# A two-layer graph network on 128 graphs: the last B round of each quad on ScalarE and GpSimd

## What is computed

```python
def L0(x, adj, W1, b1, W2, b2):
    mask = (adj > 0.0)
    W1a, W1b = W1[:F], W1[F:]
    diff = x[:, :, None, :] - x[:, None, :, :]
    h = relu((x @ W1a)[:, :, None, :] + diff @ W1b + b1)     # 192 wide
    hm = einsum('bjkh,bjk->bjh', h, mask)
    return hm @ W2 + mask.sum(-1)[..., None] * b2
def L1(h, A, ...):
    m = relu(relu(h @ W1 + b1) @ W2 + b2)
    msg = relu(einsum('bij,bjh->bih', A, m))
    r, z = sigmoid(i_r + h_r), sigmoid(i_z + h_z)            # of msg @ W_ih, h @ W_hh
    return (1 - z) * tanh(i_n + r * h_n) + z * h
x = layernorm(x + L0(x, adj, ...))
x = layernorm(x + L1(x, adj, ...))
```

## Time and profile before

| | us |
|---|---|
| median of 3 runs | 966.77 (965.92 to 966.85) |
| the profiled execution | 966.09 |
| its span, first to last instruction | 964.4 |
| TensorE busy | 852.2 (88%) |
| VectorE busy | 870.5 (90%) |
| ScalarE busy | 568.0 (59%) |
| GpSimd busy | 314.7 (33%) |
| mean granted TensorE clock | 0.976 of full speed (1.00 in the stages) |

### The profile page before, as it was taken

How to read it: one execution, slowest core, us unless ns; L and a number is a source line. 1 busy time by engine, 2 the same in 40 slices (tenths; PEclk the granted TensorE clock), 3 DMA queues, 4 the chain that set the end, 5 groups by cost and what they waited for, 6 DMA issues and landing times.

```text
span 964.4 us, 24987 instructions
## 1 busy us (share of the span) xinstructions
PE 852.2 (88%) x10132; PEld 597.0 (62%) x10132; DVE 870.5 (90%) x1055; ACT 568.0 (59%) x1627; POOL 314.7 (33%) x300
## 2 busy tenths in 40 slices
PE   2678788999999898999999898999989899999983
PEld 1345566666666666666666666676666666666652
DVE  5389999999999999999999999999999999998742
ACT  3433454576666766566666657576666657656442
POOL 1111121241524324242523425142433424242441
PEclk9779999999999999999999999999999999999986
DMA  4122121213113131212113131311213121211000
GB/s 135 27 51 73 45 78 44 67 41 87 45 28 82 45 89 45 73 46 60 47 45 89 46 87 35 84 46 37 70 45 89 45 73 45 56 33 42 1 12 23
DMA packets 31425, 53.27 MB, mean 55 GB/s; under 512 B 8137, under 2 KB 16972, under 8 KB 31308
## 3 DMA queue, kind: packets, MB, share of 16 engines
q1 hardware_dynamic: 31308, 51.65, 21.3%
HBM read 13.87 MB, written 4.19 MB: 19 GB/s over the span
## 4 chain that ended last, share of the span: by engine, by line
PE 59%; DVE 23%; issue 14%; ACT 2%; POOL 1%; POOLq 0%; DVEq 0%
PE PS L772 15%; PE PS L781 11%; DVE AC L1094 8%; DVE AC L1083 5%; DVE DM L1061 4%; PE PS L826 3%; PE PS L625 3%; PE PS L838 3%; PE PS L855 3%; PE PS L646 2%; PE PS L758 2%; DVE SI L1039 2%; PE PS L612 2%; PE PS L570 1%; PE PS L637 1%
## 5 line engine op out<-in xcount | busy, mean ns | idle before, releaser
L1083 DVE SCALAR_TENSOR_TENSOR AC<-PS,AC 128x1152 f32<-128x1152 f32 (+1 forms) x288 | 350.0, 1215 | 28.3 <-PE PS L781 19.4
L1094 DVE SCALAR_TENSOR_TENSOR AC<-PS,AC 128x1152 f32<-128x1152 f32 (+1 forms) x288 | 350.1, 1216 | 23.6 <-PE PS L772 21.9
L772 PE MATMUL PS<-DM,VA 128*128 128x192 fp8e5 (+1 forms) x1152 | 134.7, 240 | 23.8 <-DVE AC L1083 21.5
L772 PE MATMUL PS<-DM,VB 128*128 128x192 fp8e5 (+1 forms) x1152 | 135.1, 240 | 0.0
L781 PE MATMUL PS<-DM,VB 128*64 128x192 fp8e5 (+1 forms) x1152 | 95.3, 244 | 38.0 <-DVE AC L1094 37.4
L1537 POOL TENSOR_TENSOR AC<-AC,NNB 128x512 f32<-128x512 f32 x64 | 76.9, 1221 | 125.4 <-DVE DM L1061 68.7
L772 PEld LDWEIGHTS PS<-DM,VA 128*128 128x128 f16 x1152 | 87.8, 100 | 48.2 <-DVE AC L1083 38.3
L781 PEld LDWEIGHTS PS<-DM,VB 128*64 128x64 f16 x1152 | 47.2, 108 | 97.2 <-issue 61.3
L781 PE MATMUL PS<-DM,VA 128*64 128x192 fp8e5 (+1 forms) x1152 | 98.4, 251 | 0.0
L772 PEld LDWEIGHTS PS<-DM,VB 128*128 128x128 f16 x1152 | 75.4, 98 | 36.8 <-issue 0.2
L1061 DVE TENSOR_SCALAR DM<-CW 128x1536 uint16<-128x1536 uint16 (+1 forms) x132 | 95.4, 764 | 0.0
(11 more groups left out here) (221 smaller groups left out, 1863.5 us busy)
## 6 DMA issues: line engine op xcount, KB each, us to landing
CW<-WM SPq DMA_DIRECT2D x128, 160.0 KB, 2.8
AT<-in_adjt SPq DMA_DIRECT2D x16, 512.0 KB, 4.6
VA<-VN SPq DMA_DIRECT2D x64, 96.0 KB, 2.2
VB<-VN SPq DMA_DIRECT2D x64, 96.0 KB, 2.2
XN<-in_xn SPq DMA_DIRECT2D x16, 256.0 KB, 4.6
out<-YO SPq DMA_DIRECT2D x15, 256.0 KB, 4.8
cs<-in_cst SPq DMA_DIRECT2D x1, 550.5 KB, 3.6
out<-YO SPq DMA_DIRECT2D x2, 128.0 KB, 1.7
```

The source lines that it names most:

```text
L772: last = e.matmul(PS[:, b + i % 2, 256 * (i // 2) + cols.start:256 * (i // 2) + cols.stop], lhs[:, GRAPH[i], 0:128], d[:, i, :], start=Fal ...
L1083: e.scalar_tensor_tensor(dst, tiles(PS[:, b:b + 3, :])[:, :, cols], 0.0, dst, ALU.max, ALU.add).then_inc(s["sx"], 1)
L1094: e.scalar_tensor_tensor(dst, tiles(PS[:, b:b + 3, :])[:, :, cols], 0.0, dst, ALU.max, ALU.add).then_inc(s["sy"], 1)
```

## The change

Round B9 of quads 0 to 30 leaves VectorE. ScalarE writes the relu of the three banks to a new buffer RT (semaphore rb), and GpSimd adds RT to AC (semaphore acc). RT is single, so ScalarE's next read waits for GpSimd's last addition. sy counts eight for each quad from now on (nine for the last quad, whose B9 stays on VectorE); the seed matmuls wait for rb, out0_a for acc. NNB becomes bf16. The dense path uses RT in place of NNB[0]. Both rows of ORDER are new; LAST isn't changed.

```diff
 ORDER = (
-    ("ps2p3", "pe", "t", "t", "", "dtr", "e", "pdrpe", "", "ert", "pee", "ep", "4d", "p", "pre", "", "cwpd", "r", "e01"),
-    ("sp2d3", "pp", "", "t", "d", "tpp", "", "4tept", "n", "dp", "d", "p", "dc", "nld", "d0wpd", "", "epd", "p", "d1r"),
+    ("p2sep3", "", "p", "t", "rde", "tec", "", "dpptr", "", "ert", "eep4", "d", "", "ep", "pe", "d", "rp", "pr", "w01e"),
+    ("spd2", "pp3", "", "d", "t", "ptp", "", "4tptn", "e", "ldcp", "d", "p", "d", "nwdp", "", "d", "pd", "0d", "erd1p"),
 )
...
-        NNB = [sb(f"NNB{i}", [128, 6, 128]) for i in range(2)]
+        NNB = [sb(f"NNB{i}", [128, 6, 128], BF16) for i in range(2)]
+        RT = sb("RT", [128, 6, 128])
...
             def seeds(q):
                 b, x = 3 * (q % 2), XE[q % 4]
-                pe.wait_ge(s["sy"], 9 * (q - 1))
+                pe.wait_ge(s["rb"], q - 1)
...
             def round_b(q, n):
...
-                    pe.wait_ge(s["sy"], 9 * q + n - 1)
+                    pe.wait_ge(s["sy"], 8 * q + n - 1)
...
             def out0_a(q, b, gates):
                 ac = AC[q % 3]
-                pe.wait_ge(s["sy"], 9 * q + 9)
+                if q < NQ - 1:
+                    pe.wait_ge(s["acc"], q + 1)
+                else:
+                    pe.wait_ge(s["sy"], 8 * q + 9)
...
             def round_b(q, n):
+
+                if n == 9 and q < NQ - 1:
+                    return
                 b = 3 * (q % 2)
                 ve.wait_ge(s["gy"], 9 * q + n)
...
+            def round_b(q, n):
+                if n == 9 and q < NQ - 1:
+                    b = 3 * (q % 2)
+                    ac.wait_ge(s["gy"], 9 * q + 9)
+                    ac.wait_ge(s["acc"], q)
+                    e.activation(RT[:], tiles(PS[:, b:b + 3, :])[:, :, nat], ACT.Relu).then_inc(s["rb"], 1)
+
...
+            def round_b(q, n):
+                if n == 9 and q < NQ - 1:
+                    t = tiles(AC[q % 3][:])[:, :, nat]
+                    po.wait_ge(s["rb"], q + 1)
+                    po.wait_ge(s["sy"], 8 * q + 8)
+                    e.tensor_tensor(t, t, RT[:], ALU.add).then_inc(s["acc"], 1)
```

More of the change, by code:

```diff
@@ L322, in layer1_steps @@
                 if u == NG and k:
-                    step(*(("gate_h", 0), ("gate_h", 1), ("gate_hn",))[k - 1], k - 1, [("sy", 9 * NQ)])
+                    step(*(("gate_h", 0), ("gate_h", 1), ("gate_hn",))[k - 1], k - 1, [("sy", 8 * NQ + 1), ("rb", NQ - 1)])
                 yield
@@ L327, in layer1_steps @@
                 step("gt", 2, [])
-                step("gate_in", 3, [("sy", 9 * NQ)])
+                step("gate_in", 3, [("sy", 8 * NQ + 1), ("rb", NQ - 1)])
                 step("gt_in", 3, [])
@@ L817, in s_ov @@
                 ac = AC[q % 3]
-                pe.wait_ge(s["sy"], 9 * q + C1)
+                pe.wait_ge(s["sy"], 8 * q + C1)
                 for name, v in gates:
@@ L912, in out0 @@
                     e.matmul(o, XT[:, p, :], BDC[:, 64 * a:64 * a + 64], start=True, stop=False)
-                    e.matmul(o, NNB[0][:, a, :], w2s[:, 0, :], start=False, stop=False)
-                    last = e.matmul(o, NNB[0][0:64, 2 + a, :], w2s[0:64, 1, :], start=False, stop=True)
+                    e.matmul(o, RT[:, a, :], w2s[:, 0, :], start=False, stop=False)
+                    last = e.matmul(o, RT[0:64, 2 + a, :], w2s[0:64, 1, :], start=False, stop=True)
                 last.then_inc(s["o0"], 1)
@@ L1090, in round_b @@
                 else:
-                    ve.wait_ge(s["sy"], 9 * q + n - 1)
+                    ve.wait_ge(s["sy"], 8 * q + n - 1)
                 cols = back if n <= C1 else nat
@@ L1434, in scalar_main @@
             follow(main_order, {"rank_n": rank_n, "split_x": split_x, "ov": ov, "rank_t": rank_t, "rank_ov": rank_ov, "x_turn": x_turn,
-                                "v": v, "v_low": v_low, "surplus": surplus, "seeds": seeds, "s_ov": s_ov, "out0_c": out0_c,
+                                "v": v, "v_low": v_low, "surplus": surplus, "seeds": seeds, "round_b": round_b, "s_ov": s_ov, "out0_c": out0_c,
                                 "fold": fold,
@@ L1449, in stp @@
                 ac.wait_ge(s["o0"], p)
-                e.activation(NNB[0][:, 0:2, :].rearrange("p i n -> p (i n)"), PS[:, b, 0:256], ACT.Copy)
-                e.activation(NNB[0][0:64, 2:4, :].rearrange("p i n -> p (i n)"), PS[0:64, b, 256:512], ACT.Copy).then_inc(s["stc"], 1)
+                e.activation(RT[:, 0:2, :].rearrange("p i n -> p (i n)"), PS[:, b, 0:256], ACT.Copy)
+                e.activation(RT[0:64, 2:4, :].rearrange("p i n -> p (i n)"), PS[0:64, b, 256:512], ACT.Copy).then_inc(s["stc"], 1)
             follow(dense_order, {"products": products, "stp": stp, **scalar_layer1(e, ac, s, PG)})
@@ L1537, in seeds @@
                     e.tensor_tensor(t[:, h, nat], t[:, h, nat], NNB[q % 2][:, h, :], ALU.mult).then_inc(s["im"], 1)
+            def round_b(q, n):
[4 more added lines that the diff above has]
+                    e.tensor_tensor(t, t, RT[:], ALU.add).then_inc(s["acc"], 1)
             def dgen(t, m):
                 po.wait_ge(s["dd"], RD * t + m + 1)
-            follow(main_order, {"setup": setup, "split_x": split_x, "split_xg": split_xg, "clear": clear, "seeds": seeds, "dgen": dgen, **gpsimd_layer1(e, po, s)})
+            follow(main_order, {"setup": setup, "split_x": split_x, "split_xg": split_xg, "clear": clear, "seeds": seeds, "round_b": round_b, "dgen": dgen, **gpsimd_layer1(e, po, s)})
         def gpsimd_dense(e):
```

## The result

The changed kernel took 971.11 us (median of 5 runs, 970.12 to 972.80) against 966.85 for the kernel before (5 runs): a ratio of 1.0045, 95% interval 1.0031 to 1.0060. It is slower by 4.3 us, where 19 us less had been forecast; 971.1 lies outside the range of 936 to 964. The profiled execution took 970.12 us, its span 968.2.

The account below looks back on a forecast made before the run. VectorE was taken to bound even stages, TensorE to be nearly full in odd ones. 15 even stages x 1.05 and 15 odd x 0.3 gave -20.3 us, rounded to -19 for hand-overs: 947.5 us, range 936 to 964.

Parts of the forecast that it names:

- Which engine bounds which stage: Stages of alternating B and A rounds: VectorE bounds even ones, TensorE spare 2.5 us; odd ones leave TensorE 0.64 us.
- Round B9, the two new operations: B9 off VectorE saves 0.87 us per quad; ScalarE's read takes 0.81 us, GpSimd's addition 1.8.
- The decodings move: Stage boundaries: even to odd, the 1.07 us hold shrinks to 0.3 to 0.7; odd to even, seed multiplication holds none.
- The sum, even stage: Each even stage: -0.87 for B9, about -0.4 shorter hold, +0.2 gaps, making -1.05 us; bounds -0.4 to -1.6.
- rival 1: GpSimd's addition holds VectorE's last count operations after A8; even stages gain nothing; 962 us; chance 0.21 with rival 4.
- rival 4: TensorE takes over fully: odd stages 0, even -0.4 us, near 960 us; chance 0.21 together with rival 1.
- The sum, odd stage: Each odd stage: 18.6 us up to A8, then 8.0 to 8.5 to A1; 26.85 taken, -0.3 us.
- Rival 3: Stage boundaries: A1 waits for GpSimd's seed multiplication, so slower, 973 us (968 to 985); chance 0.12.
- Counts in bf16: GpSimd's seed multiplication: at best 0.15 us saved each, at worst nothing; taken as nothing.

Follow-up runs that it names:

- e5: Changed kernel with GpSimd's addition of RT cut from 768 columns to 8, so its result isn't the kernel's; 946.6 us, ratio 0.9800.
- e7: Changed kernel, B9 given away only by quads whose B rounds run in even stages, addition waiting for the last count operation; 947.1 us, ratio 0.9801.
- e2: Kernel before with the two new ORDER rows alone; B9 stays on VectorE, counts stay in float32; 953.8 us, ratio 0.9865.
- e6: Kernel before with the surplus counts in bf16 alone (and buffer RT for the dense path); 963.6 us, ratio 0.9967.
- e4: Changed kernel with one more GpSimd wait: in even stages the addition of RT waits for the last count operation; 956.5 us, ratio 0.9891.
- e1: Changed kernel with the ORDER rows of the kernel before, leaving B9's move and the bf16 counts; 1005.1 us, ratio 1.0403.
- e3: Changed kernel with the count step moved in the even row from after A8 to after A7; 973.3 us, ratio 1.0070.

## Why the prediction was wrong

- *Which engine bounds which stage*: right as far as it went. TensorE's share in the odd stage was read and then not used in full. e5 and e7 show that VectorE's 0.87 us are worth nothing there.
- *Round B9, the two new operations*: right. The read takes 0.81 us at its median, the addition 1.81; 0.81 and 1.8 had been worked out.
- *The decodings move*: right. No decoding is held at the even to odd boundary, where 0.3 to 0.7 us of hold had been left, and at the odd to even one the hold is by the gate addition. The prediction had no number for the rows alone; e2 gives 13 us for them.
- *The sum, even stage* (-1.05): this is the step that failed. +0.22 was measured. The term that failed is the hold of a count operation by the addition, for which the sum has nothing. The hold of line 1035, 1.62 us, was described as rival 1, with the right group of operations and the right mechanism, and given 0.21 together with rival 4. It was held small by the argument that an addition started 1.5 us after A8 would meet early count operations only. It started 2.04 us after A8 (602.75 to 604.79), of which the read's start was 1.16, and the operations of lines 1034 and 1035 began 2.01 and 2.09 us after A8. The prediction's own working could have said so: it put the addition's start 1.5 to 2.5 us after A8 and the end of the last count operations at 2.3, so the order was open, and a mechanism that costs 1.6 us on one side of it needed more than 0.2. Without the hold the term would have been -0.74 (27.71 to 26.97), mis-sized by 0.3: the gaps were put at 0.2 us, and B1 alone waits 1.05 us for TensorE.
- *The sum, odd stage* (-0.3): +0.10 was measured. Up to A8 it is 18.87 us against 18.6. From A8 to A1 it is 8.41 against 8.5: taking turns was right, the mask's hold was short, the dgen's behind the gate addition was long. The value was chosen between two ends, 26.6 and 27.1; the stage takes 27.28, so the upper one was the better, and both were short.
- *Rival 1*: the mechanism was right, the price 962 us wrong. It left the even stage at no change and kept a gain in the odd one. Neither held.
- *Rival 3*: A1 does wait for the multiplication, 0.51 us, but that doesn't decide: it waits 0.52 in e2, which is 17 us faster than the changed kernel. The measured 971.1 lies in this rival's range (968 to 985) by chance; its mechanism was not what made the loss.
- *Counts in bf16*, taken as nothing: 2.6 to 3 us in the kernel before (e6).

So the change is two changes that go against each other. The new rows give 13 us, the move of B9 costs 17. By pair of stages, the one 8-column instruction that was held by the addition costs 0.96 us (e4) and the addition at the odd to even boundary 0.76; the move in even stages gives back 0.31 and the bf16 counts 0.17. That sums to 1.24 us, and from e2 to the changed kernel the pair grew by 1.22 (0.64 and 0.58). Over 15 pairs that would be some 18 us, where the medians lie 17.3 apart: the first and the last stages differ less.

## What to carry to other kernels

Time taken off the busiest engine is worth what the other engine of the lockstep leaves in that very stage: 27 us of VectorE were worth 5 (0.31 us in each even stage, nothing in the odd ones). When work goes to GpSimd, list every VectorE instruction that will run beside it and reads two inputs from SBUF or is a tensor_scalar, the smallest too, and see to it that none of them starts while the long one runs, by its place or by one wait on GpSimd. When a change has parts that can stand alone, time them alone: here one was a clear gain and hid under the loss of the other.

## What the runs showed of the hardware

- An 8-column tensor_tensor of VectorE took 1.79 us in place of 0.16 when it started 0.05 us after a 1.81 us GpSimd addition; its neighbour, a 16-column tensor_scalar that started 0.03 us before the addition, took 0.17.
- The hold ends with the running GpSimd instruction; with three of 0.7 us, two VectorE instructions in a row were held for 0.5 us each.
- A tensor_reduce beside the same addition wasn't held (0.16 us), nor was a tensor_tensor beside an 8-column GpSimd power instruction of 1.67 us.
- TensorE's granted clock fell to 1.2 GHz behind seven of twelve waits of 2.23 us (e1) and two of thirteen waits of 1.00 us (e3), for 3.4 or 6.8 us each time; such a fall cost 1.3 to 2.9 us.
